# Interleaving a graph-attention kernel's setup with its first group, and a first round whose context is a mask times a vector

## The reference

```python
x_loc = ents                                   # (32, 128, 128)
x_ctx = jnp.broadcast_to(init_mem, ents.shape) # one row for every token
var_drop = ent_mask[:, :, None]                # (32, 128, 1)
for t in range(4):
    cmd = _lin(q_base, w_qt[t], b_qt[t])
    xc = x_ctx * var_drop
    pl = _lin(x_loc, w_pl, b_pl)
    pc = _lin(xc, w_pc, b_pc)
    x_joint = jnp.concatenate([x_loc, xc, pl * pc], axis=-1)
    q = _lin(x_joint, w_q, b_q)
    k = _lin(x_joint, w_k, b_k) * _lin(cmd, w_pk, b_pk)[:, None, :]
    v = _lin(x_joint, w_v, b_v) * _lin(cmd, w_pv, b_pv)[:, None, :]
    # for each of 4 edge types i: s = (q @ w1)[:, :, None] + (k @ w2)[:, None, :], kept where adj == i
    e = jnp.where(edge_score > 0, edge_score, ALPHA * edge_score)
    prob = jax.nn.softmax(jnp.where(adj_pos, e, -9e15), axis=-1)
    message = jnp.einsum('bij,bjd->bid', prob, v)
    x_ctx = _lin(jnp.concatenate([xc, message], axis=-1), w_mu, b_mu)
return _lin(jnp.concatenate([x_loc, x_ctx], axis=-1), w_cb, b_cb)
```

## Time and profile before

| what | us |
|---|---|
| median of three runs | 610.03 (607.51 to 610.65) |
| the profiled execution's own time | 610.83 |
| its span | 608.2 |
| TensorE busy | 522.2 |
| VectorE busy | 442.5 |
| ScalarE busy | 391.0 |
| GpSimd busy | 269.2 |

### The profile page before, as it was taken

One profiled execution on the slowest core, in us unless ns is written; L12 is line 12 of the kernel. 1 busy time (PEld: TensorE's weight loads), 2 busy tenths in 40 slices (PEclk: granted clock), 3 DMA queues, 4 the chain that ended last, 5 costly groups with the idle time before them and its releaser, 6 DMA issues. The chain is left out here.

```text
span 608.2 us, 14434 instructions
## 1 busy us (share of the span) xinstructions
PE 522.2 (86%) x4679; PEld 345.5 (57%) x4679; DVE 442.5 (73%) x1175; ACT 391.0 (64%) x1095; POOL 269.2 (44%) x490
## 2 busy tenths in 40 slices
PE   5967999999999999989799888888897777777780
PEld 3555677666667666654455555554555455665660
DVE  4977688888888888857455777686968867955562
ACT  2522787878887888886576675757565564655660
POOL 0770122232322223020533547676767453756563
PEclk9999999999999999999999999999999997889896
DMA  8500699999991000000100000101050024234310
GB/s 366 219 2 2 181 293 295 301 295 305 301 299 55 0 0 1 1 1 5 33 1 2 2 10 20 37 19 54 13 181 28 27 79 118 84 101 108 103 41 8
DMA packets 48191, 60.65 MB, mean 100 GB/s; under 512 B 2416, under 2 KB 45429, under 8 KB 47366
## 3 DMA queue, kind: packets, MB, share of 16 engines
q1 hardware_dynamic: 45350, 53.57, 30.1%
q0 software_dynamic: 2784, 6.37, 3.0%
HBM read 18.29 MB, written 42.09 MB: 99 GB/s over the span
## 5 line engine op out<-in xcount | busy, mean ns | idle before, releaser
L1422 DVE TENSOR_REDUCE nm<-SC 128x8 f32<-128x1024 f32 x64 | 75.3, 1218 | 29.8 <-PE SC L945 29.6
L1341 DVE TENSOR_REDUCE room_w<-SC 128x512 f32<-128x2048 f32 x32 | 73.3, 2291 | 11.6 <-PE SC L814 11.6
L1915 ACT ACTIVATE room_p<-ST 128x1024 f32<-128x1024 f32 x64 | 61.9, 1020 | 18.1 <-PE ST L963 18.1
L542 POOL TENSOR_TENSOR spread<-parts,units 128x48 bf16<-128x48 bf16 x32 | 8.9, 277 | 144.8 <-DVE parts L1331 144.8
L1828 ACT ACTIVATE room_w<-room_w,shift 128x128 f32<-128x128 f32 x128 | 49.7, 389 | 21.3 <-DVE shift L1348 21.3
L711 POOL DMA_INDIRECT out<-room_v,id_r x39 | 38.9, 996 | 27.1 <-DVE room_v L1775 20.5
L1819 ACT ACTIVATE room_w<-ST,cv 128x128 f32<-128x128 f32 x128 | 36.5, 367 | 18.9 <-PE ST L829 18.9
L1922 ACT ACTIVATE room_w<-SC 128x512 f32<-128x512 f32 x32 | 19.1, 598 | 43.7 <-PE SC L982 39.2
L617 POOL DMA_INDIRECT sorted_rows<-room_w,slot_i x32 | 32.9, 1029 | 23.9 <-issue 18.0
L829 PEld LDWEIGHTS ST<-room_w 128*128 128x128 f32 x256 | 33.3, 191 | 16.2 <-issue 15.4
L958 PE MATMUL ST<-room_v,room_w 32*128 32x512 f32 x256 | 36.5, 638 | 6.3 <-issue 4.7
(11 more groups left out here) (275 smaller groups left out, 1379.3 us busy)
## 6 DMA issues: line engine op xcount, KB each, us to landing
sorted_rows<-w SPq DMA_DIRECT2D x8, 4290.0 KB, 38.4
room_v<-sorted_rows SPq DMA_DIRECT2D x39, 130.0 KB
ctx_t<-adj SPq DMA_DIRECT2D x1, 2048.0 KB, 10.7
x_t<-xT SPq DMA_DIRECT2D x1, 2048.0 KB, 15.1
room_w<-mask SPq DMA_DIRECT2D x1, 2048.0 KB, 19.5
room_w<-x SPq DMA_DIRECT2D x8, 256.0 KB, 2.7
w<-weights SPq DMA_DIRECT2D x1, 1292.0 KB, 6.3
x_t<-w SPq DMA_DIRECT2D x1, 1032.0 KB, 5.3
```

What stands on the lines that cost most here:

```text
L1341: dve.tensor_reduce(logit[:, :, :], SC[:, :, :].rearrange("p b (i m) -> p b m i", i=TYPES), AX_X, ALU.max)\
L1422: dve.tensor_reduce(nm[:, v % 2, 2 * PER_R * pair:2 * PER_R * (pair + 1)], SC[:, 2 * pair:2 * pair + 2, :].rearrange("p r (i n) -> p (r i) ...
L1915: act.activation(ex[:, v % 2, 2 * pair:2 * pair + 2, :], ST[:, 2 * pair:2 * pair + 2, :], ACT.Exp)\
```

## The change

It does six things. (1) `xT` and the mask are loaded in pieces, ahead of the adjacency, and the weight columns of `pl` come with the first piece of weights. (2) The `pl` products (`local`), the x values and the penalties are taken apart by group or by half and written between the stages of groups 0 to 3. (3) In round 0 the context is never formed. Five small products make the vectors of the first round from `init_m` (`v_row`, `key_row`, `mu_row`, `pc_col`); `v_product` then multiplies 32 rows of the mask with them, in two products per batch of 132 and 4 columns where there was one of 136; the update multiplies `mu_row` with the mask. (4) The products `pc` and `pl_times_pc` of round 0 are gone; GpSimd's `first_products` makes `plpc` of steps 0 to 7 instead, in two instructions. (5) The first round is written out and the loop runs over rounds 1 and 2. (6) The experts' bias is split on GpSimd over eight partitions and brought into place by two DMAs through memory.

```diff
-            with eng.Fori(0, T_ITER - 1) as t:
+            for g in range(G):
+                step(0, g)
+            with eng.Fori(1, T_ITER - 1) as t:
                 for g in range(G):
                     step(t, g)
...
             sp.dma_start(w[:, 0:NW_FIRST], weights[:, 0:NW_FIRST]).then_inc(in_w, 16)
+            sp.dma_start(x_t[:, 0:HALF], xT[:, 0:HALF]).then_inc(in_x, 16)
             sp.dma_start(cst[:, :], consts).then_inc(in_c, 16)
             sp.dma_start(w[:, NW_FIRST:NW], weights[:, NW_FIRST:NW]).then_inc(in_w2, 16)
+            sp.dma_start(x_t[:, HALF:TOK], xT[:, HALF:TOK]).then_inc(in_x2, 16)
+            sp.dma_start(mask_b[:, 0:2 * GT], mask[:, 0:2 * GT].broadcast_to([128, 2 * GT])).then_inc(in_mask, 16)
+            sp.dma_start(rowv[:, :], rowvecs.broadcast_to([128, NR])).then_inc(in_bv, 16)
             sp.dma_start(adj_s[:, :], adj).then_inc(in_adj, 16)
...
+            def first_products(g):
+
+                cols = slice(g * GT, (g + 1) * GT)
+                if g < 2:
+                    pool.wait_ge(in_mask, 16)
+                    pool.wait_ge(vx_mm, 2 * g + 2)
+                else:
+                    pool.wait_ge(v_done, g - 1)
+                    pool.wait_ge(in_rest, 48)
+                pool.tensor_scalar(plpc[:, g % 2, :], mask_b[:, cols], pc_col[:, 0:1], bias("pc"), ALU.mult, ALU.add)\
+                    .then_inc(S("pc_ready"), 1)
+                pool.wait_ge(S("pc_ready"), g + 1)
+                pool.wait_ge(pl_done, g + 1)
+                pool.tensor_tensor(plpc[:, g % 2, :], plpc[:, g % 2, :], pl_t[:, cols], ALU.mult).then_inc(plpc_done, 1)
...
             for k in range(2, 5):
                 pool.wait_ge(v_done, k - 1)
                 key_columns(0, k)
                 place(k - 1)
+                first_products(k)
+                add_bias(k)
+                if k == 2:
+                    bias_parts()
+            pool.memset(pad_row, 0.0).then_inc(S("spread_ready"), 1)
+            pool.wait_ge(S("spread_ready"), 4 + TYPES)
+            pool.memset(pad_row[:, 2 * D + 1:2 * D + 2].bitcast(I32), FAR).then_inc(S("spread_ready"), 1)
+            pool.wait_ge(pen_done, 2 * TYPES)
...
                 if ahead(t, g, 4):
                     place(s + 4)
-                if not isinstance(t, int):
+                if opens(s) and opens(s + 5):
+                    first_products(s + 5)
+                    add_bias(s + 5)
+                if not closing(t):
                     pool.wait_ge(t_done, s + 4)
                     masked_context(s, t, g)
...
-                for b in range(GB):
-                    pe.matmul(V[:, b, 0:D + QK], ctx_t[:, g * GT + b * N:g * GT + (b + 1) * N],
-                              w_v[:, g % 2, b, 0, :], start=b in (0, 3), stop=False)
+                if opens(s):
+                    for b in (0, 3, 1, 2):
+                        at, cols = slice(STRIP * (b // 3), STRIP * (b // 3 + 1)), slice(g * GT + b * N, g * GT + (b + 1) * N)
+                        keys = slice((g * GB + b) * TYPES, (g * GB + b + 1) * TYPES)
+                        pe.matmul(V[:, b, 0:D + TYPES], mask_b[at, cols], v_row[at, :], start=b in (0, 3), stop=False)
+                        pe.matmul(V[:, b, D + TYPES:D + QK], mask_b[at, cols], key_row[at, keys], start=False, stop=False)
...
-                if ahead(t, g, 5):
+                if ahead(t, g, 5) and not opens(s + 5):
                     pc(s + 5, (g + 5) % G, s + 2)
...
+            def penalties_of(half, i):
+
+                bs = slice(half * B // 2, (half + 1) * B // 2)
+                dve.wait_ge(in_adj, 16)
+                dve.tensor_scalar(penalty[:, bs, i, :], adj_s[:, half * HALF:(half + 1) * HALF].rearrange("p (b m) -> p b m", m=N),
+                                  float(i + 1), -BIG, ALU.not_equal, ALU.mult).then_inc(pen_done, 1)
...
                 if ahead(t, g, 2):
                     inverse(s + 2)
-                if ahead(t, g, 5):
+                if isinstance(s, int) and s == 0:
+                    penalties_of(1, 2)
+                    penalties_of(1, 3)
+                if ahead(t, g, 5) and not opens(s + 5):
                     pl_times_pc(s + 5, (g + 5) % G)
```

More of the change, by code:

```diff
@@ L105, in shape_constants @@
     at["tile"][:] = np.arange(40)
-    for n in range(1, NPART):
-        at["less"][n:, n - 1] = -1.0
     return c
@@ L413, in rounds, with closing, opens @@
                 step(T_ITER - 1, g)
+        def closing(t):
+            return isinstance(t, int) and t == T_ITER - 1
+        def opens(s):
+            return isinstance(s, int) and s < G
         def ahead(t, g, k):
@@ L724, in _, with local @@
                 mm = pe.matmul(M0[:, t, 0:B], W("qt", t), q_base[:, :], start=True, stop=True)
-            mm.then_inc(cmd_mm, 1)
+            mm.then_inc(setup_mm, 1)
+            def local(g):
+                if g >= 2:
+                    pe.wait_ge(pl_done, g - 1)
+                pe.wait_ge(in_x if g < G // 2 else in_x2, 16)
+                pe.matmul(TB[g % 2][:, :, :].rearrange(flat), W("pl"), x_t[:, g * GT:(g + 1) * GT],
+                          start=True, stop=True).then_inc(pl_mm, 1)
@@ L726, in _, with x_values @@
+            def x_values(g):
+                for b in range(g * GB, (g + 1) * GB):
+                    if b % 2 == 0 and b >= GB:
+                        pe.wait_ge(vx_act if b % GB == 0 else vx_dve, b // GB)
+                    mm = pe.matmul(VX[:, b % GB, 0:D + TYPES * (1 + T_ITER)], x_t[:, b * N:(b + 1) * N], w_x[:, b, :],
+                                   start=True, stop=True)
+                    if b % 2:
+                        mm.then_inc(vx_mm, 1)
+            local(0)
             pe.wait_ge(cmd_ready, T_ITER)
@@ L757, in _ @@
+            local(2)
+            fold(1, PT0)
             pe.wait_ge(wx_ready, 1 + T_ITER)
             pe.wait_ge(wv_const, 4)
-            for b in range(B):
-                if b % 2 == 0 and b >= GB:
-                    pe.wait_ge(vx_act if b % GB == 0 else vx_dve, b // GB)
-                mm = pe.matmul(VX[:, b % GB, 0:D + TYPES * (1 + T_ITER)], x_t[:, b * N:(b + 1) * N], w_x[:, b, :],
-                               start=True, stop=True)
-                if b % 2:
-                    mm.then_inc(vx_mm, 1)
+            x_values(0)
@@ new lines, in _ @@
+            pe.wait_ge(fold_ready, 1)
+            fold(2, M0)
+            pe.wait_ge(in_c, 16)
+            pe.wait_ge(ckw2_ready, 2)
+            pe.wait_ge(fold_ready, 2)
+            pe.matmul(PT0[:, :, :].rearrange(flat), C("ones"), bk_w2[:, :], start=True, stop=True).then_inc(setup_mm, 1)
+            pe.wait_ge(S("u_out"), 1)
+            pe.wait_ge(bqw1_ready, 1)
+            pe.matmul(PC0[:, 0:TYPES], C("ones"), bq_w1[:, :], start=True, stop=True).then_inc(setup_mm, 1)
+            pe.wait_ge(cmd_ready, CV_OUT)
@@ L768, in pc @@
+            x_values(1)
             def pc(s, g, evac):
-                pe.wait_ge(ctx_done, s + 1)
-                if not (isinstance(s, int) and s == 0):
-                    pe.wait_ge(plpc_done, s)
+                pe.wait_ge(ctx_done, s + 1 - G)
+                pe.wait_ge(plpc_done, s)
                 pe.wait_ge(S("u_out"), evac)
@@ L844, in _ @@
             pe.wait_ge(kbias_ready, 1)
-            pc(0, 0, 1)
+            pe.wait_ge(S("first_ready"), 1)
+            pe.wait_ge(msg_evac, 1)
+            pe.wait_ge(in_mask, 16)
             pe.wait_ge(S("wv_query"), 2)
+            x_values(2)
+            v_product(0, 0)
+            x_values(3)
+            local(3)
+            pe.wait_ge(consts_ready, 1)
+            turn_parts(0)
+            x_values(4)
+            v_product(1, 1)
+            x_values(5)
+            x_values(6)
+            x_values(7)
+            for g in range(4, G):
+                local(g)
+            pe.wait_ge(pl_done, G)
             pe.wait_ge(vx_act, B // GB)
             pe.wait_ge(vx_dve, B // GB)
-            v_product(0, 0)
-            pc(1, 1, 1)
-            pe.wait_ge(consts_ready, 1)
-            turn_parts(0)
-            v_product(1, 1)
-            pc(2, 2, 1)
-            pe.wait_ge(pl_done, G)
             pe.wait_ge(pen_done, TYPES)
-            pe.wait_ge(msg_evac, 1)
             penalties(0, 0)
@@ L1853, in context @@
                 else:
-                    act.wait_ge(ctx_done, G + s)
+                    if not (isinstance(s, int) and s == 0):
+                        act.wait_ge(ctx_done, s)
                     act.wait_ge(mu_done, s + 1)
                     act.activation(ctx_raw[:, :], U[:, :], ACT.Identity, bias=bias("mu")).then_inc(S("u_out"), 1)
-            act.wait_ge(cv_ready, 1)
+            act.wait_ge(cmd_ready, CV_OUT)
             parts_turned(0)
+            for g in range(4, G):
+                x_values_out(g)
+            for g in range(4, G):
+                local_out(g)
             parts_turned(1)
```

297 lines of the change are left out of this document (165 added, 132 removed).

## The result

The changed kernel takes 616.91 us (median of 20 runs, 609.0 to 621.99); the kernel before took 608.25 on the same chips (20 runs, 604.35 to 611.05). The ratio is 1.0088, interval 1.0058 to 1.0118; it leaves out executions more than 1.5% above the fastest of their kernel, nine of the 20 of the changed one, which is why it is less than the ratio of the medians, 1.014. The change made the kernel slower, by more than the 0.5% that I took as the limit of what can be told. I had forecast 606.2, in a range from 602 to 612.5.

The account below looks back on a forecast made before the run. TensorE bounds the full pipeline; ahead of it a chain through the engines counts one for one. -6.8 - 1.8 + 2.7 + 1.7 = -4.2 us on 610.83 gives 606.6, from the median 605.8; taken 606.2, range 602 to 612.5.

Parts of the forecast that it names:

- The setup: Everything up to the first reduction: it would start at 43.4 us instead of 50.21, -6.8 us.
- First reduction to step 2's: Two chained cycles through all engines: 14.2 us for 16.06, without the earlier half-clock stretch, -1.8 us.
- the rival of the long half clock: Setup gaps before step 2 bring some 14 us at half clock: +7 us, so 613; chance 0.14.
- The other half-clock rival: Clock falls in the new 4 us gap ahead of `turn_parts(4)`: next step 2.7 us longer, 608.9; chance 0.27.
- The wait for the penalties: GpSimd waits for all eight half penalties before step 0's `place(4)`; TensorE gap about 4 us, step 3 later: +2.7 us.
- Steps 0 to 3: Round 0 steps take 7.56 us for 7.06 in three steps, and a rest of 0.2 in the fourth: +1.7 us.
- GpSimd's longer piece: 3.3 us more between `place` and masked context in round 0, delaying ScalarE's context copy: 0.3 to 0.6 us a step.
- Costed at nothing: Experts' bias moved off VectorE (already in the -6.8), the loop's boundary with round 0 written out, and the padding DMAs.
- My bounds of 1.28 and 1.76: New value product's first half, in us: least if strips overlap wholly, most if passes are serial; 1.5 taken, 0.93 before.

Follow-up runs that it names:

- again: The changed kernel once more, without an edit: 597.84 us, ratio 1.0113 to the kernel before.
- rows32_pen_order_fill: Changed kernel, still 32 rows, with penalty wait moved to step 4, value bias behind the masked context, 23 idle products in setup gaps: 605.62 us, ratio 0.9903.
- full_rows: Changed kernel with all 128 rows instead of 32 in the first round's products with the mask: 591.60 us, ratio 1.0011 to the kernel before.
- busy_fill: Changed kernel with 30 products nobody reads in TensorE's gaps of the setup and step 0: 587.01 us, ratio 0.9918 to the kernel before.
- pen_later: Changed kernel with GpSimd's wait for all eight half penalties moved from step 0 to step 4's masked context: 594.78 us, ratio 1.0045.
- before_unrolled: The kernel before with only round 0 written out ahead of the loop: 611.82 us, ratio 1.0006.
- before_fill: The kernel before with 20 products nobody reads in the gaps of its own setup: 589.06 us, ratio 0.9946.
- full_pen: Changed kernel with 128 rows in the products with the mask and GpSimd's penalty wait moved to step 4: 588.40 us, ratio 0.9951.

## Why the prediction was wrong

**The setup** (-6.8): right. 43.02 for 43.4, 7.2 us gained; x products and first penalties came 1.8 and 0.5 us ahead of my figures. Part of that is that TensorE reached full speed near 12 us, where I had said 14: a pair of passes of 512 columns took 1.85 us at 8.25 and 0.86 at 12.41.

**First reduction to step 2's** (14.2 us, -1.8): this is where it failed. It took 17.6 us in the change's profile and 19.1 in again's. With 32 rows and the clock held it takes 14.05 (rows32_pen_order_fill, 42.91 to 56.96), so the 14.2 was a sound sum for full clock; the excess is half clock, which the sum left out. It even counted the kernel before's one half-clock stretch as a gain of 1.8, as if the change could only remove such stretches.

**The step that failed** is the sentence against the rival of the long half clock: "the stretch before, 51 to 54.8, had like gaps and kept its clock". On it the sum put half clock behind the setup's gaps at nothing, and the rival got 0.14. These are the windows of the kernel before that lie ahead of those of the earlier trace rows:

```profile
41.20:44.60 3.40, 1.78 (x12) 0.98 (x11) 2.94 (x9) 0.00 (x0) 0.64 (x3) 1.00 0.01 2
44.60:48.00 3.40, 2.46 (x22) 2.26 (x21) 0.29 (x2) 0.70 (x1) 0.00 (x0) 1.00 0.00 0
48.00:51.40 3.40, 2.13 (x29) 0.75 (x28) 3.26 (x8) 0.70 (x1) 0.64 (x3) 1.00 0.00 0
51.40:54.80 3.40, 3.40 (x38) 2.15 (x37) 3.23 (x10) 0.88 (x5) 0.00 (x0) 1.00 0.02 5
```

In the stretch that I named TensorE was busy throughout; there were no like gaps in it. The three windows ahead of it do have gaps, and they kept the clock. So the argument could have been made with the right rows, and it would have failed all the same: the changed kernel lost its clock behind a window with more work in it (2.62 of 3.50 us, 42.8 to 46.3). What made the gaps unlike were the products between them. Before, all f32 products had 128 rows; now the first halves of the value products and of the context updates have 32, and giving those 128 rows, with the gaps left as they were, took 6.2 us off the time (full_rows). The prediction had weighed the 32 rows only for what a pass costs.

I had the long half clock right as a mechanism and in size (7 us for 14 us of it; again had 17.1 and 13.7 us, the change 10.2 twice). The other half-clock rival, the gap ahead of the fifth turn, had 0.27 and 2.7 us; it came as well, and lasted 10.2 us instead of one stretch. I had set the two as alternatives, and both came. By busy_fill against again they cost together 10.8 us. With the clock mostly held, the change has the ratio 0.9918 (0.9889 to 0.9948) for the 0.9937 that I forecast: apart from half clock the sum stood, as a total.

**The wait for the penalties** (+2.7): right in kind, and nearly in size. The gap was 3.69 us, and step 3's reduction came 9.70 us after step 2's, 2.1 more than before. That pen_later is 3.1 us below again does not measure it, since the gap moved and the half clock changed with it.

**Steps 0 to 3** (+1.7): the size was right (7.60 and 7.72 between steps 4 and 6), the cause for these steps was not. GpSimd's longer piece does hold ScalarE's copy up by 2.08 us, as I said, but moving the bias behind the masked context left them at 7.8 and 7.9. They are long because the value product is dearer and the product by `w_pc` had lain in a wait that stays without it. The sums agree, if the 0.86 of that product is not taken off: 7.06 and 0.50 more for the first half (1.43 for 0.93) make 7.56, and with 128 rows, 1.71 for 0.93 in these steps, they make 7.84. Only from step 3 to step 4 did the order on GpSimd cost something, 0.9 us once the wait was moved.

**Costed at nothing**: the loop written out is nothing (before_unrolled). The experts' bias was not tried apart.

**What stays open**: how rows and gaps weigh together in the clock. The 32 rows mattered with the gaps open (full_rows against again) and no longer did once the gaps were filled. I can show that either cure works, not what the chip counts. busy_fill's profile also shows that the changed kernel can lose its clock as early as 30 us, ahead of every fill; that stretch was not taken apart. The rule of the Trainium skill that I cited for the clock ("TensorE: Matmul & The Clock Gate", Part 1), that idleness throttles and work releases, agrees in its direction with before_fill, where filling the gaps left no half clock of the 3.4 us.

## What to carry to other kernels

Taking work out of a chain, or spreading it between the stages of another, also thins TensorE's work; look at the granted clock of every stretch ahead of the full pipeline, and price a half-clock stretch of some 10 us behind each cluster of gaps where the products take few rows (10.2 to 17.1 us in most cases here), not the 3.4 us that every stretch lasted with 128 rows. Where gaps of about 1 us can't be avoided, a few products that nobody reads, or products with all 128 rows instead of 32, can be worth more than the work saved: here the same change went from 1.011 to 0.987 or 0.989 of the time before by fills, full rows, a wait moved behind the first work that needs it, and one reordering. And before work is counted as removed from a step, see whether the engine waits at that place for something else; before a wait is moved, see what will then run beside it, and what the next wait in the chain is.

## What was not expected of the hardware

- At the same busy time (2.5 of 3.4 us) the granted clock fell with products of 32 rows and held with 128, shown above. In the changed kernel it then stayed at 0.50 for 10.2 us (70.2 to 80.4) although TensorE was busy throughout, by its modelled ends; with 128 rows it came back after 3.4 us behind the same gap (full_rows).
- Fewer rows do make a product of few columns cheaper where two batches stand in different strips: 1.40 for 1.78 us in the value product's first half. My bounds of 1.28 and 1.76 had left this open. The Trainium skill's rule that a weight load goes by its columns ("TensorE: Matmul & The Clock Gate", LDWEIGHTS) agrees with the 1.78 of 128 rows, and by itself does not give the 1.40. There the eight passes of the two batches in different strips took 0.44 us together (44.06 to 44.50), as much as the four of the next batch alone (to 44.94): the strips overlap wholly.
- VectorE and GpSimd slow each other. From the timelines of both in the changed kernel's setup:

```profile
25.55 2.17 POOL L562 TENSOR_TENSOR room_w<-room_w,room_v 128x512 f32<-128x512 f32 x1
...
30.22 1.21 POOL L543 COPY room_w<-room_w 128x32 f32<-128x32 f32 x1
...
26.74 1.02 DVE L1404 CAST parts<-qk 128x32 bf16<-128x32 f32 x1
...
28.02 0.18 DVE L1411 CAST parts<-res 128x32 bf16<-128x32 f32 x1
...
29.48 1.89 DVE L1367 TENSOR_SCALAR room_p<-ctx_t 128x2048 bf16<-128x2048 int32 x1
```

The cast at 26.74 lies beside GpSimd's product, which ends at 27.7, and takes 1.02 us; the one at 28.02 has no such neighbour and takes 0.18. GpSimd's copy at 30.22 lies beside penalties and takes 1.21, where the same copy took 0.21 at 68.67. In the setup this cost nothing that the first reduction shows. In pen_later and full_pen it did cost: there the tensor-scalar beside two penalties took 2.92 us for 0.77, and TensorE waited at the end of that chain.
- The granted clock of the windows reads 1.00 from the start of both kernels, also while TensorE still ran at half speed (the pairs of passes above, 1.85 us at 8.25 and 0.86 at 12.41). For the first microseconds the time of a pass tells the clock, not that column.
